# Two more latent tiles turned by DVE and DRAM, one memory addition and two weight parts moved to later places

## The reference

```python
x = x + _L0_attn_ref(_layernorm(x), Wq, bq, Wk, bk, Wv, bv, Wo, M, z)[0]
    # q = (xn @ Wq.T + bq) in heads of 128;  sig_q = elu(q) + 1;  every fourth head
    # retrieved = (sig_q @ M) / (sig_q @ z + 1e-6);  out = repeat(retrieved, 4) @ Wo.T
x = x + _L0_xattn_ref(_layernorm(x), ctx, Wq, Wk, Wv, Wo)
    # latents = the normalised x; keys and values of concat(ctx, latents);
    # 32 query heads over 4 key heads, softmax, @ Wo
x = x + _L0_ffn_ref(_layernorm(x), router_w, router_b, expert_b)
    # softmax router over 64, top 8, x * sum(w) + w @ expert_b
```

## Time and profile before

| | |
|---|---|
| time, median of 3 runs | 671.48 us |
| the profiled execution, its own time | 671.39 us |
| its span in the trace | 669.5 us |
| PE busy (matmuls) | 659.2 us, 98% |
| DVE busy | 515.3 us, 77% |
| ACT busy | 402.1 us, 60% |
| POOL busy | 143.8 us, 21% |
| DMA, mean | 183 GB/s |
| chain that ended last | PE 81%, DVE 8%, DMA 3%, ACT 3% |

### The profile page before, as it was taken

One profiled execution on the slowest core, in us unless ns is written; L12 is line 12 of the kernel. 1 busy time (PEld: TensorE's weight loads), 2 busy tenths in 40 slices (PEclk: granted clock), 3 DMA queues, 4 the chain that ended last, 5 costly groups with the idle time before them and its releaser, 6 DMA issues.

```text
span 669.5 us, 11116 instructions
## 1 busy us (share of the span) xinstructions
PE 659.2 (98%) x3322; PEld 553.9 (83%) x3322; DVE 515.3 (77%) x1101; ACT 402.1 (60%) x1224; POOL 143.8 (21%) x150
## 2 busy tenths in 40 slices
PE   8999999999999999999999999999999999999997
PEld 6888778877888888888888888888888888888885
DVE  3774879998788887767867976777877676778887
ACT  4455765654553456676677767766875575555543
POOL 0196122334332311211011011010110000032422
PEclk9999999999999999999999999999999999999999
DMA  9997154652743656788775669867667673322101
GB/s 335 369 362 270 54 169 124 160 140 61 232 148 127 203 170 211 193 271 240 239 225 174 193 190 274 263 182 212 210 197 212 205 244 95 91 78 64 58 22 63
DMA packets 113636, 122.70 MB, mean 183 GB/s; under 512 B 7536, under 2 KB 83568, under 8 KB 113584
## 3 DMA queue, kind: packets, MB, share of 16 engines
q1 hardware_dynamic: 108656, 114.22, 55.4%
q10 hardware_dynamic: 4928, 7.87, 3.2%
HBM read 78.54 MB, written 43.52 MB: 182 GB/s over the span
## 4 chain that ended last, share of the span: by engine, by line
PE 81%; DVE 8%; DMA 3%; ACT 3%; issue 2%; SPq 2%; POOL 1%; DVEq 0%; ACTq 0%
PE bank L1180 25%; PE bank L1251 24%; PE bank L997 10%; PE bank L1374 8%; PE bank L1391 6%; DMA sig_dram<-rawk 2%; PE bank L988 2%; PE bank L1150 2%; DVE kvout L2132 2%; SPq L644 1%; PE bank L1400 1%; PE bank L1038 1%; PE bank L1320 1%; DVE rawk L2119 1%; ACT probs L1820 1%
## 5 line engine op out<-in xcount | busy, mean ns | idle before, releaser
L1251 PE MATMUL bank<-regA,oT 128*128 128x512 f32 x576 | 135.2, 390 | 1.2 <-DVE oT L2004 1.2
L1820 ACT ACTIVATE probs<-bank,negmax 128x128 f32<-128x128 f32 x256 | 90.0, 377 | 68.9 <-DVE negmax L2485 65.7
L1251 PEld LDWEIGHTS bank<-regA,oT 128*128 128x128 f32 x576 | 107.8, 188 | 24.0 <-DVE oT L2004 1.8
L1180 PE MATMUL bank<-xnT,forms 128*128 128x512 f32 x432 | 107.1, 392 | 0.0
L1180 PEld LDWEIGHTS bank<-xnT,forms 128*128 128x128 f32 x432 | 80.2, 188 | 16.2 <-DVE qbuf L2242 0.2
L1180 PE MATMUL bank<-regC,forms 128*128 128x512 f32 x324 | 82.5, 393 | 0.0
L1180 PEld LDWEIGHTS bank<-regC,forms 128*128 128x128 f32 x324 | 59.9, 188 | 12.0 <-DVE regC L2004 0.2
L997 PE MATMUL bank<-regC,xnT 128*128 128x512 f32 x256 | 67.0, 392 | 0.0
L923 POOL TENSOR_TENSOR diff<-wq_raw 128x256 f32<-128x256 f32 x15 | 11.9, 796 | 253.0 <-DVE forms L2004 253.0
L1374 PEld LDWEIGHTS bank<-k_ring,qbuf 128*128 128x128 f32 x512 | 62.0, 191 | 2.5
L1502 ACT CAST oT<-bank 128x512 fp32r<-128x512 f32 (+1 forms) x66 | 37.6, 575 | 42.1 <-PE bank L1391 36.6
(11 more groups left out here) (219 smaller groups left out, 1164.1 us busy)
## 6 DMA issues: line engine op xcount, KB each, us to landing
q_dram<-qbuf SPq DMA_DIRECT2D x32, 512.0 KB, 3.5
qbuf<-q_dram SPq DMA_DIRECT2D x31, 512.0 KB, 5.2
turns_dram<-probs SPq DMA_DIRECT2D x88, 128.0 KB, 2.5
pT_raw<-turns_dram SPq DMA_DIRECT2D x22, 512.0 KB, 5.0
wq_raw<-in_L_xattn_Wq SPq DMA_DIRECT2D x14, 512.0 KB, 4.6
raw<-in_L_attn_Wo SPq DMA_DIRECT2D x6, 1024.0 KB, 8.2
raw<-in_L_xattn_Wo SPq DMA_DIRECT2D x12, 512.0 KB, 6.1
k_ring<-keys_dram SPq DMA_DIRECT2D x32, 128.0 KB, 4.5
```

Source lines behind the costliest of these rows:

```text
L1180: last = nc.tensor.matmul(k_bank[:, :], forms[:, p[1], a, i, c, :], right(b)[:, c, :], start=j == 0, stop=j == 5)
L1251: last = nc.tensor.matmul(bank[7][:, :], oT[:, a, h, :], wo_of(g, b, h), start=h == 0 and i == 0, stop=h == GH - 1 and i == 2)
L1820: last = nc.scalar.activation(dst, keys, ACT.Exp, bias=negmax[:, bb, p:p + 1], accum_out=rowsum[:, bb, p:p + 1])
```

## The change

- `LAT_TURNED` goes from 5 to 7. Latent tiles 5 and 6 are turned by DVE and go through DRAM; only tile 7 is transposed by PE, between value products 2 and 3 as before. ACT's high parts of tiles 5 and 6 stand behind the saves of value products 0 and 2; that of tile 7 stands behind the save of value product 3, where it stood behind that of product 2. POOL's low parts of tiles 5 and 6 stand behind all memory steps and ahead of the form sums. PE's value product 6 waits for POOL's low part.
- `added_in` replaces `output_in` where x is added to: tile 4 is added in step 15, in place of 14. Its root and its scaling move with it.
- SP issues the load of the second key weights (`k_raw`) behind latent tile 4 and ahead of tile 5's stores; it stood last. The load of the first output weights (`wo_raw`) waits for seven latents in place of five.
- The low parts of output heads 6 and 7 move from the end of `step_turned(2, 6)` to behind the maxima of `step_between`.

```diff
-        LAT_TURNED = NT - 3
+        LAT_TURNED = NT - 1
...
-        def latent_on_pe(i):
-
-            t = (output_in(i) or 0) - 1
-            return t if LAT_TURNED <= t < NT - 2 else None
...
+        def added_in(i):
+
+            late = (4,)
+            if output_in(i) in late:
+                return None
+            return output_in(i - 1) if output_in(i - 1) in late else output_in(i)
...
             for t in range(3, LAT_TURNED):
+                if t == NT - 3:
+                    sp.wait_ge(sig_tr_done, 2 * NT - SIG_TURNED)
+                    sp.dma_start(k_raw, wk_rows[:, :, 2 * P:4 * P]).then_inc(k_raw_loaded, 16)
                 store_latent(t)
                 load_latent(t)
             sp.wait_ge(lat_lo, LAT_TURNED)
             sp.wait_ge(wkv_lo, 3 * KC)
             sp.dma_start(wo_raw, wo_rows[:, 0:GH, :]).then_inc(wo_loaded, 16)
-            sp.wait_ge(sig_tr_done, 2 * NT - SIG_TURNED)
-            sp.dma_start(k_raw, wk_rows[:, :, 2 * P:4 * P]).then_inc(k_raw_loaded, 16)
...
-                if output_in(i) is not None:
-                    root(2 + output_in(i))
+                if added_in(i) is not None:
+                    root(2 + added_in(i))
                 if latent_in(i) is not None:
...
+                    latent_low(latent_in(i))
+            for t in range(NT - 3, LAT_TURNED):
+                latent_low(t)
...
                 values(mm("vlat", t), wkv2, xn_cols, t)
-                if t in (0, 2):
-                    latent_transposes(NT - 2 + t // 2)
+                if t == 2:
+                    latent_transposes(NT - 1)
...
             for t in range(NT - 1):
                 save_latent_values(t)
                 if t in (0, 2):
-                    latent_high(NT - 2 + t // 2)
+                    loaded_high(NT - 3 + t // 2)
+                if t == 3:
+                    latent_high(NT - 1)
...
-                if i and output_in(i - 1) is not None and output_in(i - 1) < LAT_TURNED:
-                    turn_latent(output_in(i - 1))
-                if latent_on_pe(i) is not None:
-                    x_low(tr("latent", latent_on_pe(i)), latent_on_pe(i))
-                if output_in(i) is not None:
-                    add_memory(output_in(i))
+                if added_in(i - 1) is not None and added_in(i - 1) < LAT_TURNED:
+                    turn_latent(added_in(i - 1))
+                if added_in(i) is not None:
+                    add_memory(added_in(i))
...
-            x_low(tr("latent", NT - 2), NT - 2)
             dve.wait_ge(lat_lo, NT // 2)
...
-                if at(g, t, 2, 6):
-                    wo_low(KV - 1, GH - 2)
-                    wo_low(KV - 1, GH - 1)
...
                 for bb in range(2):
                     maxima(n, bb)
+                wo_low(KV - 1, GH - 2)
+                wo_low(KV - 1, GH - 1)
                 wo_low(KV - 1, 0)
```

More of the change, by code:

```diff
@@ L902, in _, with latent_low @@
                 nc.gpsimd.tensor_tensor(folded(m), w[:, :, 0, :], w[:, :, 1, :], ALU.add).then_inc(fold_done, 1)
+            def latent_low(t):
+                pool.wait_ge(lat_hi, t + 1)
+                nc.gpsimd.tensor_tensor(latT_place(1, t), latT_source(t), latT_place(0, t).bitcast(F),
+                                        ALU.subtract).then_inc(lat_lo, 1)
             for i in range(2 * NT + 5):
@@ L1133, in memory_step @@
                     wo_transposes(i + EARLY)
-                if latent_on_pe(i) is not None:
-                    latent_transposes(latent_on_pe(i))
             def memory_output(s):
@@ L1657, in _, with loaded_high @@
                 save_key(mm("kctx", i), NT + i, 0, i)
+            def loaded_high(t):
+                act.wait_ge(lat_loaded, 16 * t + 16)
+                high(latT_place(0, t), latT_source(t)).then_inc(lat_hi, 1)
             def latent_high(t):
@@ L1702, in _ @@
                 if latent_in(i) is not None:
[L1703 to L1707, removed]
+                    loaded_high(latent_in(i))
             def save_latent_values(t):
@@ L2119, in memory_step @@
                     nc.vector.transpose(sig_turns(s), sig[:, s % 3, :]).then_inc(sig_turned, 1)
-                if i and output_in(i - 1) is not None:
-                    scale_latent(output_in(i - 1))
+                if added_in(i - 1) is not None:
+                    scale_latent(added_in(i - 1))
                 if 1 <= i <= 2 * NT:
@@ L2170, in scale_latent @@
                 if t >= 2:
-                    if t - 2 < LAT_TURNED:
-                        dve.wait_ge(lat_turned, t - 1)
-                    else:
-                        dve.wait_ge(tr_done, tr("latent", t - 2) + 1)
+                    dve.wait_ge(lat_turned, t - 1)
                 src, dst = resid[:, t, :], xn[:, t % 2, :]
```

4 lines of the change are left out of this document (removed).

## The result

The changed kernel takes 675.08 us (median of 15 runs, 673.62 to 675.51); the kernel before, in the same job, 671.48 (15 runs, 670.25 to 673.66). The ratio is 1.0042, 95% interval 1.0033 to 1.0051: slower by 2.2 to 3.4 us. The ratio is the one that goes with the interval; the two medians lie 3.6 us apart. The forecast was 673.4, slower, range 670.9 to 674.8. The ratio on the 671.48 of before gives 674.3, inside it; the median of the 15 runs lies 0.3 above it.

A forecast was written before the change was run, and what follows sets the result against it. TensorE, 98% busy, was taken to bound the kernel. 2.9 us lost at tile 7 (both earlier savings inside) less 0.9 for output weights gave +2.0 on 671.39: 673.4 us, range 670.9 to 674.8.

The forecast's parts named there:

- ACT's high part of tile 7: Behind value product 3's save, it makes the DVE chain 2.99 us late and TensorE 2.9 late at 195, savings included.
- the stretching that I took as 0.3: DVE's block sum after tile 7's low part may run into POOL's form sums: up to 0.87 us, taken as 0.3.
- the 0.1 that I took off: Ahead of the product at 195.23, DVE itself had waited 0.1 us, the only slack at its fourth sum.
- The tail: Last memory steps, tile 4 added one step later: o12 earlier, o14 nearly unchanged; gain 0.05 us, bounds 0 and 3.0.
- Of the 2.2 us nothing is left: In the memory tail, o12 wins 2.2 us, but o14 and the first latent values start within 0.1 us of before.
- Tiles 5 and 6: Turned through DRAM, they arrive in time, with 1.5 us cover for tile 6; POOL's subtractions ahead of its form sums are free.
- 0.47 a tile: TensorE saving for each block of PE transposes removed: 0.47 us, at most 0.94 for two tiles.
- Output weights: At 545 us, two low parts moved behind the maxima remove a TensorE wait: 0.9 us gained, bounds 0 and 1.2.
- nothing waits before 547: TensorE behind 195: no wait before 547 us, so nothing gives back the 2.9 us lateness.
- The DVE chain: Rival: DVE's sums are no date for TensorE, through slack or tile 7 in time; only gains count, 669.6 us; chance 0.10.
- tile 6 was not late: Opposing rival: tile 6 lands late from DRAM and stops ACT before its high part; 674.9 at 3 us late; chance 0.08.
- the relief of the tail: Rival: the memory tail is relieved in good part, everything from product 3 earlier by 0.7 to 3.0 us; chance 0.27.

The follow-up runs named there:

- b_high7: Kernel before, with only ACT's high part of latent tile 7 moved behind the save of value product 3: 675.42 us, ratio 1.0055.
- a_no_wo: Changed kernel with the low parts of output heads 6 and 7 back at the end of step_turned(2, 6): 675.39 us, ratio 1.0051.
- a_spin: Changed kernel with 20 transposes into an unread bank on TensorE ahead of the first pair product: 673.45 us, ratio 1.0023.
- b_add: Kernel before, with only the addition of tile 4 moved to step 15 in place of 14: 673.21 us, ratio 1.0018.
- a_high7: Changed kernel with ACT's high part of tile 7 back behind the save of value product 2: 674.52 us, ratio 1.0042 against the kernel before.
- a_fix: Changed kernel with tile 7's high part back behind value product 2's save and POOL's pair 0 form sums ahead of tile 6's low part: 672.67 us, ratio 1.0006.
- c_five: Changed kernel with tiles 6 and 7 on PE as before, tile 5 by DRAM, no late addition of tile 4: 670.43 us, ratio 0.9975 against the kernel before.
- b_wo: Kernel before, with only the two low parts of output weights moved behind the maxima of step_between: 672.67 us, ratio 1.0001.
- a_no_add: Changed kernel with the addition of tile 4 back in step 14: 673.55 us, ratio 1.0018 against the kernel before.

## Why the prediction was nearly right

**ACT's high part of tile 7: the mechanism was right, the term too small.** The forecast put DVE's low part at 177.43, then no gap, a TensorE wait of 2 us for the save of product 6, and 2.9 at 195. Seen: 178.40 with 0.47 of it lead, the wait 2.00 for that save, and 3.87. b_high7 shows the cause with no other edit, if with a longer DMA wait on the way. The step that failed is the last sentence of the term, that nothing but DVE's lateness acts behind 187: the wait itself can bring the clock down, and no price for that stood in the sum. Of the 0.97 over the forecast 0.48 arises between the first low part of the chain (3.37 late net) and the fourth sum (3.85), where DVE in its turn waits 0.54 for the slow matmuls. Product 3 is another 0.33: it was to start 0.40 earlier than before and starts 0.07 earlier. Its save comes 0.17 later behind it than I had put it. Against that, the stretching that I took as 0.3 is 0.18 (178.40 to 189.55 is 11.15, before 10.97), and the 0.1 that I took off for a wait of DVE's own is not given back.

In a_no_wo and a_spin, with the same order at this place and the full clock, the delay is 2.62 and 2.56. That 2.9 lies between these and 3.87 is in part luck, since product 3 starts at 172.60 and 172.53 net there and at 173.21 in the changed kernel: the forecast of 172.88 falls between the two by the tail's scatter. How often the clock falls at this place is not known. 9 of the 15 executions have the lower mean clock, but a mean does not say where it fell, and 7 of 35 executions of the kernel before have one too.

**The tail: the steps came as dated.** o12 was forecast at 150.1 and came at 151.03, 150.56 net; the transposes of sigma 15 at 154.7 (155.17 net; 154.47 net in a_spin); the scaling stretched to 1.4 (1.43). o14 was to start at 158.7 and starts at 159.50, 159.03 net, behind a wait of 0.43 for DVE: this is the 0.3 by which product 3 is later than forecast. "Of the 2.2 us nothing is left" holds in b_add. In a_high7, a_fix and a_spin o12 is at 149.8 to 150.1 net. POOL held DVE in one more place in the profile of the change, at the last of sigma 14's denominators (1.40 where its neighbours take 0.28), where I had named the small instruction behind it. The tail's own scatter of some 0.5 us is larger than what I argued over.

**Tiles 5 and 6.** The DRAM way was in time for both, as forecast. That POOL's subtractions are free was wrong: a_high7 and a_fix show that tile 6's, ahead of the form sums, is a date about as tight as ACT's. It did not show in the changed kernel, since tile 7 was later still. 0.47 a tile was right (0.49 in c_five).

**Output weights.** -0.9 forecast, -0.89 seen, and -0.90 in b_wo.

**What the sum did not have.** Two small delays behind 195 (0.42 by 240 us and 0.26 from there to 300; in the other profiles the two together are -0.01 to 0.45), which "nothing waits before 547" had excluded. With them the account in the profile is 3.87 + 0.68 - 0.89 = 3.66, and 0.1 more to the end, on a lead of 0.47: 4.2, the difference of the spans. By the ratio the loss is 2.8 us, by the medians 3.6, by the forecast 2.0.

**The rivals.** The DVE chain was a date; tile 6 was not late; the relief of the tail did not reach o14. Each was told apart by the row that the prediction named for it. A rival that was not thought of, a second date hidden behind the first, is the one that decides whether the idea of seven tiles could be saved: repaired in both, it gives 1.0006, so it is not a gain even then.

## What to carry to other kernels

Work taken off the bound engine is worth its price only if the other engines' dates stand still: a cast of 0.6 us one save further back cost more than eight transposes and a wait gave. When a date is missed, look for the second one right behind it before undoing the first; here POOL's queue had one. A wait of some 2 us on TensorE should be counted with the matmuls behind it, which ran at the lower clock in part of the executions (0.6 to 0.7 us here). A change of 0.1% is read from the distance of the two timelines at fixed matmuls, taken between a place just ahead of the change and one behind it, not from medians.

## What the hardware showed unexpectedly

The granted clock fell behind a single wait of 2.00 (changed), of 2.03 (a_no_add) and of 2.39 us (b_high7), though TensorE had run without a recorded wait from 159.50 to that wait in the first, and in b_wo behind two waits of 0.71 and 1.19 with 0.66 us of transposes between; the rows of matmuls then take 2.4 for 1.5 us and 4.6 for 3.0. It is not certain to fall: a_no_wo had a wait of 2.03 and a window from 186 to 194 us at 1.00, where the changed kernel has 0.79, and the profile of a_high7 kept 1.00 behind its wait of 2.36. Twenty transposes into an unused bank kept it up in all 12 runs.

POOL and DVE lengthen each other in both ways: DVE's scaling of 0.55 takes 1.43 and a denominator of 0.28 takes 1.40 beside POOL's subtraction of 1.28, and POOL's sums of 0.74 take 1.6 to 1.7 beside DVE's sums.
